# Expert rows in groups of 512, 512 and 256 instead of five of 256, with two staging buffers for weights

## The reference

```
logits = clip(xf @ Wr); top_v, top_i = top_k(logits, 2); top_p = softmax over the two
cap = ceil(T*K*1.25/E)                 # T = 4096 tokens, K = 2, E = 8 experts: cap = 1280
xe  = rows of xf, put by expert and by place in the expert, places from cap on dropped
h   = silu(einsum('ecd,edf->ecf', xe, W1)) * einsum('ecd,edf->ecf', xe, W3)   # d = 256, f = 1024
ye  = einsum('ecf,efd->ecd', h, W2)
out[token] += weight * ye              # two experts for each token
```

## Time and profile before

| what | us |
|---|---|
| median of 3 runs | 1486.77 |
| lowest and highest | 1482.56, 1491.43 |
| the profiled execution | 1484.94 |
| its span, first to last instruction | 1482.9 |

### The profile page before, as it was taken

One profiled execution on the slowest core, in us unless ns is written; L12 is line 12 of the kernel. 1 busy time (PEld: TensorE's weight loads), 2 busy tenths in 40 slices (PEclk: granted clock), 3 DMA queues, 4 the chain that ended last, 5 costly groups with the idle time before them and its releaser, 6 DMA issues. The chain is left out here.

```text
span 1482.9 us, 32499 instructions
## 1 busy us (share of the span) xinstructions
PE 1366.7 (92%) x10841; PEld 1214.5 (82%) x10841; DVE 951.4 (64%) x3162; ACT 633.6 (43%) x1596; POOL 346.0 (23%) x524
## 2 busy tenths in 40 slices
PE   6899999899999999999848999999999999999995
PEld 4677777777777767767628999999999999999995
DVE  5577888787887778778654556455554545555442
ACT  2444554454554444444324435344443434444331
POOL 3113232231231322222220222122211112121122
PEclk9999999999999999999858999999999999999998
DMA  3821210100100100000003242412424142231111
GB/s 92 232 80 32 96 52 18 31 30 17 31 31 16 31 26 20 31 30 13 22 28 115 40 116 33 115 30 52 104 33 116 30 114 39 68 82 30 30 23 22
DMA packets 67292, 79.67 MB, mean 54 GB/s; under 512 B 11090, under 2 KB 60723, under 8 KB 67154
## 3 DMA queue, kind: packets, MB, share of 16 engines
q1 hardware_dynamic: 52562, 59.09, 13.1%
q0 software_dynamic: 14592, 18.91, 7.7%
HBM read 44.04 MB, written 33.96 MB: 53 GB/s over the span
## 5 line engine op out<-in xcount | busy, mean ns | idle before, releaser
L862 ACT ACTIVATE h_a<-banks 128x256 f32<-128x256 f32 x320 | 122.5, 383 | 358.0 <-PE banks L1370 355.7
L1304 DVE TENSOR_TENSOR h_f<-banks,h_a 128x256 f32<-128x256 f32 x320 | 135.6, 424 | 158.9 <-ACT h_a L862 150.2
L506 POOL TENSOR_TENSOR idle_g<-half 128x1 f32<-128x1 f32 x144 | 29.3, 203 | 703.4 <-DVE y_s L1323 396.8
L1370 PE MATMUL banks<-xe_t_hi,w_even_hi 128*128 128x256 f32 x640 | 180.3, 282 | 0.1
L1370 PE MATMUL banks<-xe_t_hi,w_odd_hi 128*128 128x256 f32 x640 | 179.3, 280 | 0.0
L1370 PE MATMUL banks<-xe_t_lo,w_even_hi 128*128 128x256 f32 x640 | 178.4, 279 | 0.0
L1370 PE MATMUL banks<-xe_t_hi,w_even_lo 128*128 128x256 f32 x640 | 178.2, 279 | 0.0
L1370 PE MATMUL banks<-xe_t_lo,w_odd_hi 128*128 128x256 f32 x640 | 177.7, 278 | 0.0
L1370 PE MATMUL banks<-xe_t_hi,w_odd_lo 128*128 128x256 f32 x640 | 177.7, 278 | 0.0
L851 ACT ACTIVATE h_t_hi<-h_f 128x256 fp32r<-128x256 f32 x320 | 131.8, 412 | 32.0 <-DVE h_f L1304 31.8
L1311 DVE TENSOR_TENSOR h_t_lo<-h_f,h_t_hi 128x256 fp32r<-128x256 f32 x320 | 133.5, 417 | 6.1 <-ACT h_t_hi L851 5.3
(11 more groups left out here) (240 smaller groups left out, 3500.2 us busy)
## 6 DMA issues: line engine op xcount, KB each, us to landing
raw<-in_w SPq DMA_DIRECT2D x24, 1024.0 KB, 5.9
expert_rows<-empty SPq DMA_DIRECT2D x4, 2580.0 KB, 11.1
xe<-expert_rows SPq DMA_DIRECT2D x40, 258.0 KB, 2.8
xin<-in_x SPq DMA_DIRECT2D x32, 128.0 KB, 2.3
out_dram<-x SPq DMA_DIRECT2D x32, 128.0 KB, 1.9
out_dram<-y_s,token POOLq DMA_INDIRECT x80, 3.8
mask_i<-in_mask SPq DMA_DIRECT2D x32, 32.0 KB, 1.8
expert_rows<-r_xn,send POOLq DMA_INDIRECT x64, 3.1
```

The source lines that it names most:

```text
L506: return pool.tensor_tensor(idle_g[:, i:i + 1], half[:, 0:1], half[:, 0:1], ALU.add)
L862: act.activation(h_a[:, f % 2, :], bank[2 + f % 4][:, 0:GS], ACT.Silu).then_inc(silu_ok, 1)
L1304: dve.tensor_tensor(h_f[:, f % 2, :], bank[2 + f % 4][:, GS:2 * GS], h_a[:, f % 2, :], ALU.mult)\
L1370: last = pe.matmul(dst, lhs, rhs, start=(i == 0), stop=(i == len(pairs) - 1))
```

## The change

The experts' 1280 rows are taken as 512, 512 and 256, so 24 groups in place of 40. A matmul of the projections then has 512 columns in two of three groups. What one bank held (up and gate, 256 columns each) now takes two banks, and the four banks make two turns instead of four. The flipped rows take banks 0 and 1, the results up to four tiles in banks 6 and 7 together. `xe` and `y_s` hold four tiles in one buffer each (two buffers of two tiles before), `h_a` is single, and `about` turns over three. Weights have two staging buffers: w1 and w2 share `raw0`. So a w2 is loaded only after its expert's w1 is split, and in expert 0 that puts it behind the first stage's last store. The pieces are split in groups 0 and 1 of an expert, at feature tiles 2, 4 and 6.

```diff
-GS = 256
-GPE = CAP // GS
+GS = 512
+STARTS = list(range(0, CAP, GS))
+SIZES = [min(GS, CAP - r) for r in STARTS]
+GPE = len(SIZES)
...
-        raw_of = {m: sb(f"raw{m}", [P, 2, 4 * D]) for m in (1, 2, 0)}
-        raw = [raw_of[m] for m in range(3)]
+        raw1 = sb("raw1", [P, 2, 4 * D])
+        raw0 = sb("raw0", [P, 2, 4 * D])
+        raw = [raw0, raw1, raw0]
...
-        xe = sb("xe", [P, 2, 2, ROW])
+        xe = sb("xe", [P, TILES, ROW])
...
-        y_s = sb("y_s", [P, 2, 2, D])
+        y_s = sb("y_s", [P, TILES, D])
...
-            if g in (1, 2, 3) and f in (3, 6) and not is_last(e, E - 1):
-                return e + 1, (g - 1) * 2 + (f == 6)
+            if g < 2 and f in (2, 4, 6) and not is_last(e, E - 1):
+                return e + 1, g * 3 + f // 2 - 1
...
-            load_expert(0)
+            load_expert(0, (0, 1))
...
+            sp.wait_ge(w_lo_ok, 2)
+            load_expert(0, (2,))
...
-            for g in range(2):
-                load_group(g, g)
+            load_group(0, 0)
+            sp.wait_ge(xet_mm, 1)
+            sp.wait_ge(about_ok, 1)
+            load_group(0, 1)
+            sp.wait_ge(w_lo_ok, PIECES)
+            load_expert(1, (0, 1))
...
-                if j % GPE == 0 and not (isinstance(d, int) and 2 * d + j // GPE == E - 1):
-
-                    e = 2 * d + j // GPE
-                    sp.wait_ge(w_lo_ok, (e + 1) * PIECES)
-                    load_expert(e + 1)
+                if j % GPE == 0 and not is_last(e, E - 1):
+                    sp.wait_ge(w_lo_ok, (e + 1) * PIECES + 2)
+                    load_expert(e + 1, (2,))
+                if j % GPE == 2 and not (isinstance(d, int) and e + 2 >= E):
+                    sp.wait_ge(w_lo_ok, (e + 2) * PIECES)
+                    load_expert(e + 2, (0, 1))
...
-                if later(g, 2):
-                    dve.wait_ge(added, (g - 1) * 32)
+                if later(g, 1):
+                    dve.wait_ge(added, tiles_before(d, j) * 16)
...
-                    if later(n, 4):
-                        pe.wait_ge(gated_ok, n - 3)
-                    to = bank[2 + f % 4]
+                    if later(n, 2):
+                        pe.wait_ge(gated_ok, n - 1)
                     for m in range(2):
-                        last = split_product(to[:, m * GS:(m + 1) * GS], [
+                        last = split_product(bank[2 + 2 * (f % 2) + m][:, 0:rows], [
```

More of the change, by code:

```diff
@@ L1319, in results @@
                 dve.wait_ge(about_ok, g + 1)
-                for a in range(2):
-                    dve.tensor_copy(token[par][a][:, :], about[:, par, a, 0:1])
-                for a in range(2):
-                    last = dve.tensor_scalar(y_s[:, par, a, :], bank[6 + par][:, a * D:(a + 1) * D],
-                                             about[:, par, a, 1:2], None, ALU.mult)
-                last.then_inc(y_ok, 1)
-            def read_about(g, par):
-                if later(g, 2):
-                    dve.wait_ge(y_ok, g - 1)
-                dve.wait_ge(xe_landed[par], (g - par) * 8 + 16)
-                dve.tensor_copy(about[:, par, :, :], xe[:, par, :, D:ROW]).then_inc(about_ok, 1)
+                for a in range(tiles):
+                    dve.tensor_copy(token[par][a][:, :], about[:, j % 3, a, 0:1])
@@ new lines, in results, with read_about @@
+                for a in range(tiles):
+                    last = dve.tensor_scalar(y_s[:, a, :], bank[6 + a // 2][:, a % 2 * D:(a % 2 + 1) * D],
+                                             about[:, j % 3, a, 1:2], None, ALU.mult)
+                last.then_inc(y_ok, 1)
+            def read_about(d, j):
+                g, par, tiles = d * GPL + j, j % 2, rows_of(d, j) // P
+                if later(g, 3):
+                    dve.wait_ge(y_ok, g - 2)
+                dve.wait_ge(xe_landed, g * 16 + 16)
+                dve.tensor_copy(about[:, j % 3, 0:tiles, :], xe[:, 0:tiles, D:ROW]).then_inc(about_ok, 1)
@@ L1334, in _ @@
+            read_about(0, 0)
             columns(0, 0)
-            for g in range(2):
-                read_about(g, g)
             def group(d, j):
-                g, par = d * GPL + j, j % 2
+                g = d * GPL + j
                 for f in range(FT):
-                    gated(g, par, f)
+                    gated(d, j, f)
                     if f:
-                        hidden_low(g, par, f - 1)
+                        hidden_low(d, j, f - 1)
                     if f == 2 and not is_last(g, NG - 1):
-                        columns(g + 1, 1 - par)
+                        columns(*following(d, j, 1))
+                    if f == 0 and not is_last(g, NG - 1):
+                        read_about(*following(d, j, 1))
@@ L1685, in results @@
                 if j % GPE == 0:
-                    pe.wait_ge(w_lo_ok, (2 * d + j // GPE + 1) * PIECES)
-                if later(g, 2):
-                    pe.wait_ge(y_ok, g - 1)
-                for a in range(2):
-                    last = split_product(bank[6 + par][:, a * D:(a + 1) * D], [
+                    pe.wait_ge(w_lo_ok, (expert(d, j) + 1) * PIECES)
+                if later(g, 1):
+                    pe.wait_ge(y_ok, g)
+                for a in range(rows_of(d, j) // P):
+                    last = split_product(bank[6 + a // 2][:, a % 2 * D:(a % 2 + 1) * D], [
                         ([h_t[part][:, par, f, a * P:(a + 1) * P] for part in range(2)],
```

142 lines of the change are left out of this document (81 added, 61 removed).

## The result

The changed kernel takes 1521.5 us (median of 4 runs, 1518.0 to 1524.5) where the kernel before takes 1486.8: a ratio of 1.022, with a 95% interval from 1.018 to 1.026. I had forecast 1488, and a range up to 1501. The profiled execution took 1520.25 us with a span of 1518.5, 35.6 more than the span before.

A forecast was written before the change was run, and what follows sets the result against it. Entry, TensorE's stream and tail were taken to set the end; -20 + 4 + 0 + 10.5 + 4.9 + 1.5 = +1 on the profiled 1484.9 gave 1486, so 1488 as median; range 1476 to 1501.

The forecast's parts named there:

- What 512 columns save: 20: Up and gate projections: 1536 pairs of 256-column matmuls (114.6 ns each) become single ones at 216 ns, saving 20 us.
- upper end: Faster rival: wide matmuls at 213.3 ns (24 us), slow rate gone (3), stalls of 1; 1478 us, chance 0.14.
- narrow gain: Rival in the expert stage: wide matmuls at 220 ns, so only 12 us saved; chance 0.15.
- The two banks' depth: +4: 256-row groups: 1024-column copies delay gates, TensorE waits 0.5 to 0.6 us, seven times; 4 us, ends 1 and 8.
- The additions in mid-stage: 0: Expert stage: a 512-row group's output additions make VectorE wait half a microsecond, covered by two tiles in hand; 0 us.
- The tail: +10.5: After the last groups: four serial additions must land before single y_s is rewritten; end 10.5 us later, 9 to 13.
- The entry: +4.9: Expert stage start: doubled first load, second load waiting for the single xe buffer; 4.9 us later, 4 to 6.5.
- w2 of expert 0: +1.5: End of first stage: w2, loaded behind the last x2 store, delays its split and the routing 1.5 us, 0.5 to 4.
- chance of slower, 0.31: Chance of a time above 1494.2 us: most of the three slower rivals and the forecast's upper edge.

The follow-up runs named there:

- the probe: Changed kernel with added matmuls of several types and operand places behind its last results, products unread; 1762.0 us, one run, which says nothing of the layer.
- e1_shift64: Changed kernel with 64 unused bytes per partition ahead of xe_t, restoring the old relative place of xe_t and h_t; 1521.0 us, ratio 1.020.
- e11_groups256: Changed kernel with groups set back to 256 rows and 192 unused bytes ahead of xe_t, the rest of the change kept; 1519.7 us, ratio 1.022.

## Why the prediction was wrong, point by point

**What 512 columns save: 20 (ends 12 and 24). This step failed.** Up and gate of two of three groups went from a pair of 229.4 ns to one matmul of 232.5 (233.4 with each group's first step), some 5 us lost. Two links broke. The 216 was taken from rows of float32 and bf16, and both types lack the price that float32r pays (215.8 for bf16 and 216.0 for a float32 row at every place tried, against 227 to 234). That float32 streams every column twice was my reading of its time; the runs show two rows to a matmul, of 216.0 each at 256 columns. The other link is that a wide matmul is free of what the narrow one pays. That was my estimate, from the 109 ns between flips, just under the 113.4 of a matmul of 256 columns. The flips are float32, and the probe's float32 rows take about twice the columns' 106.7 and 53.3 of the estimate above (216.0 for 256, 111.7 for 128), so they showed no floor for float32r. In float32r 128 columns took 112 ns, 58 beyond their columns, and what sets that no run shows. But 320, 384 and 448 columns in float32r, at 146 to 203 ns, still take 13 to 16 beyond their columns. The 213.3 at which the upper end puts a wide matmul, its columns alone, no run shows at a granted clock of 1.00 either: float32r of 512 columns took 227.0 at the least, bf16 215.8. The number stands only on the clock of 0.50, where 256 columns took 213.3 and the changed kernel's first wide matmuls 427 each, four distances from 794.75 to 796.46. So at 0.50 the time went with the columns; at 1.00 the wide ones stand 232.5 apart, 19 beyond half of the 427.

```profile
794.75 0.63 PE L1405 MATMUL banks<-xe_t_hi,w_even_lo 128*128 128x512 f32 x1
...
796.46 0.63 PE L1405 MATMUL banks<-xe_t_hi,w_even_hi 128*128 128x512 f32 x1
```

The dear end of this step, 220 for a wide matmul and 12 us saved, is the "narrow gain" that got 0.15: the same price on a matmul of any width, 6.7 ns beyond the columns. There is a price on the wide ones, but by the estimate above it is 14 to 21 ns at 512 columns.

**The rest of the stream.** I had taken the 256-column matmuls as unchanged. This is a second term, put at nothing, that failed. They went from 114.6 to 118.7, on 2688 matmuls 11 us, where the new buffers shift `xe_t` and `h_t` from 64 to 128 bytes off the weights. The old place brings all of it back for up and gate and half of it for the way back (114.1 and 116.4 in e1_shift64); with `xe_t` at the weights' own place and `h_t` at the old one the way back is at 116.2. Nothing in the rows ahead could show that; that the rate could change at all, with no cause in sight, stood in them as the 11 slow groups.

**The two banks' depth: +4.** The hole stands where I put it, behind the gate of tile 3, but measures 0.2 us in the changed kernel and 0.4 in e1_shift64, where matmuls are back at 113 ns; a slower TensorE hides part of it. Seven times 0.2 is 1.5. Where the group size itself was undone (e11_groups256) I had the depth at 4 as well, and the holes were 20: the splits of weights, three in a group, fall into those groups, and I had counted the copies alone.

**The additions in mid-stage: 0.** Right; TensorE has no hole of them before the last group.

**The tail: +10.5.** From VectorE's first token of the last group but one: fourth addition 15.0 us later (15.25 foreseen), first one of the last group 20.3 (20.5), second 24.7 (24.8), end 33.2 (33.1). 22.6 before, so 10.6 more.

**The entry: +4.9.** Flips 3.8 after the issue (3.7), second flips 9.6 (9.4), projections 11.2 (11.0): 5.0. That the doubled load adds 0.9 was an estimate; 3.8 against the 2.83 before is 1.0.

**w2 of expert 0: +1.5.** 2.6: it landed 6.4 us after its issue, not 5.

The rest, 2.1, is the scatter of the first stage. With the distances as they came, the first term of my own sum would have read +16 (5 of wide matmuls, 11 of narrow ones) in place of -20, which puts the profiled execution at 1522 beside the 1520.25 measured: that is nearly the whole error. Of the chance of slower, 0.31, about half went to mechanisms that add a wait, and what happened adds hardly any.

## What to carry to other kernels

Price a matmul of a new size from rows of the very same type, weight load and rate of columns; a row of another type at the same width is no bound (512 columns took 215.8 ns in bf16 and 227.0 to 234.2 in float32r), and "f32" in a profile row may be two different types (256 columns: 216.0 a row in float32, 113.3 to 120.0 in float32r). When TensorE is the bound and busy all the time, look at where its two operands lie in SBUF relative to each other: for float32r, 64 unused bytes in front of a tile made the kernel before's expert stage 4.4% longer (681.8 to 711.8 us), and a change of the memory plan can move them unasked (here from 64 to 128 bytes apart, and the narrow matmuls from 114.6 to 118.7 ns). And a memory plan that halves the buffers to make room for wider work was paid at both ends of the stage, 5.0 us at the entry and 8.2 in the tail, where nothing ran beside the serial loads and additions.

## What the hardware showed that I had not expected

The distance between float32r matmuls depends on the difference of the two operands' places modulo 256 bytes: 113.3 to 120.0 ns at 256 columns, 227.0 to 234.2 at 512 in the stream's order of operands, and with single pairs of operands 4, 8 or 16 bytes apart up to 236.7. At 256 columns it isn't the difference alone: with the moving operand 64 bytes behind, both 114 and 118 were measured. Shifts of 256 bytes, 512, 1 KB and 2 KB changed nothing (5.74 us for 24 matmuls of 512 columns each time, 5.73 without a shift). The places that suit 256 columns (192: 113.3) and 512 (0: 227.0) are not the same. With 64 columns of weights in place of 128, at the same place, 512 columns took 230.0 in place of 228.5 but 256 columns took 114 in place of 120; so at 512 the price is not that of loading 128 columns of weights, and at 256 the weights have a part in it. bf16 (215.8 and 109.2) and float32 (216.0 a row) did not move with the place, and busy VectorE and ScalarE changed nothing (232.4 each time). What in the chip makes this difference, no run here shows.
